# Layer 3 of a four-layer graph-attention kernel: V's parts side by side in the value matmuls, their sum on DVE, column vectors made in the node stages, and ACT making the kinks of three tiles of four

## The chip, the core and the metric

The program runs on one core of a Trainium2 chip. Its engines are PE (matrix products), DVE (vector), ACT (scalar functions), POOL (GpSimd) and SP, which here only issues DMAs. The metric is the time of one execution on the device, in microseconds; a kernel's time is the median of several executions.

## The reference

Eight graphs of 1024 nodes with 128 features pass through four attention layers under one adjacency matrix; after each layer `x = layernorm(x + layer(x))`. Layers 0 and 1 are dot-product attention with four heads, layers 2 and 3 additive attention. The change is about layer 3 (four heads of 32 features):

```python
Wh = jnp.einsum('bnf,hfd->bhnd', x, W)
ei = jnp.einsum('bhnd,hd->bhn', Wh, a1)
ej = jnp.einsum('bhnd,hd->bhn', Wh, a2)
e = ei[:, :, :, None] + ej[:, :, None, :]
e = jnp.where(e > 0, e, ALPHA * e)          # ALPHA = 0.2
e = jnp.where(adj[None, None] > 0, e, MASK_VAL)
att = jax.nn.softmax(e, axis=-1)
h = jnp.einsum('bhij,bhjd->bhid', att, Wh)
return jax.nn.elu(h)                         # after the heads are joined
```

Layer 2 is the same with one head of 128 features. The `where(e > 0, ...)` is what this text calls the kink.

## The kernel before

**Stages.** The program goes through five node stages (`node(0)` to `node(4)`) with the attention of a layer (`heads(0)` to `heads(3)`) between them. Each engine has its own program in one block, in the order of the stages; semaphores join them, and nothing reorders at run time. A node stage works graph by graph: it finishes the layer behind, and projects for the layer ahead. For layers 2 and 3 it writes to DRAM, per graph, V in three bf16 parts (`v_d`, each part 32 features and a one, 33 columns), rows of `ei` (`row_d`) and columns of `ei` and `ej` (`col_d`). In `project`, DVE copies the columns from PSUM bank 4 in one operation (line 1309), and the next graph's transposes on PE wait for that.

**Attention.** `heads(layer)` runs over 32 units (graph and head) in layer 3. The body holds four units, so eight passes are made; the first and the last stand outside the loop. A unit has 16 tiles of 128 keys x 512 queries: two halves of queries (c), eight key blocks (j) in each. Per tile s:

- PE, `scores(s)`: a mask matmul (lines 1063 or 1068) and the matmul with `sel` (line 1070) into PSUM bank s % 4. It adds the shift of each query, which lies as a row in `qs`.
- The kink. For tiles with s % 4 in `RELU_AT[3]`, now 1 and 3, ACT writes `relu(0.8 (ei + ej))` into the bank before PE adds to it (`relu`, line 849), right behind the exponential that has read this bank. For the others DVE makes it afterwards, in `settle(s)` (line 1402): bank to `arg` (named cv in rows).
- ACT, `exps(s)` (line 875): the exponential into `part`, from cv or from the bank (ps).
- POOL, `take_low(s)` (line 332): the low half of the probability as f16 (named xc), `part` read as bf16 being the high half.
- PE, `weigh(s - 6)`: for each of four query blocks, three matmuls of the high half and two of the low half with the parts of V, 33 columns each, added into one place of 33 columns (line 1111): 20 matmuls a tile. After the last tile of a half three more per block add V's sum for rows without neighbours (line 1118).

**Once per unit.** DVE takes eight row maxima of masked scores (`take_max`, line 1370) for the units ahead, spread over the tiles by `MAX_NEXT` and `MAX_AFTER`: at tiles 1, 2 and 7, 9, 11, 13, 14, 15. At tile 4, behind settle, `find_shift` makes the next unit's shift (lines 1346, 1347) and three scaled column vectors `colx` (1348 to 1350), which settle and ACT read as operands. At tiles 6 and 14 `half_done` (1451 to 1457) waits for `weigh` of tile 15 of the unit behind or tile 7, and normalizes half a unit. SP stores a unit's output after its second half_done (line 548), then copies the next shift into `qs` with eight DMAs (`place_shift`, line 533), then loads a unit ahead with nine DMAs (line 497).

Of the kernel before, what the change touches and what calls it, by code (L numbers as in the profile page):

```python
# [25 lines left out]
F32 = mybir.dt.float32  # L26
# [4 lines left out]
ALU = mybir.AluOpType  # L31
# [3 lines left out]
P = 128  # L35
# [35 lines left out]
RELU_AT = ((), (), (1, 3), (1, 3))  # L71
# [4 lines left out]
LOADS = (9, 7, 6, 9)  # L76
# [3 lines left out]
HCHAIN = (36, 32, 52, 28)  # L80
HLEFT = (7, 4, 6, 3)
# [6 lines left out]
def build(nc, t):  # L88
    with ExitStack() as ctx:
# [18 lines left out]
        col_d = nc.dram_tensor("col_d", (GRAPHS * 8, P, BLOCKS), F32, kind="Internal").ap()  # L108
# [46 lines left out]
        colp = sb("colp", [P, 8, BLOCKS])  # L155
# [17 lines left out]
        cols = sb("cols", [P, UNROLL, 2, BLOCKS])  # L173
        colx = sb("colx", [P, UNROLL, 3, BLOCKS])
# [49 lines left out]
        s_colx = sem("s_colx")  # L224
# [110 lines left out]
        def settled_before(layer, u, s):  # L335

            if layer == 0:
                return u * (TILES // 2 * UNROLL) + s // 2
            return TILES // 2 * UNITS[0] + TILES // 2 * (UNIT0[layer] - UNIT0[2]) + u * (TILES // 2 * UNROLL) + s // 2

        def arg_at(s):
            return s // 2 % RING
# [44 lines left out]
        def _(sp):  # L387
# [31 lines left out]
            def node(stage):  # L419
# [17 lines left out]
                def store_parts(b):  # L437
# [7 lines left out]
                    else:  # L445
                        n = 2 * HEADS[stage]
                        sp.wait_ge(s_ev["row2"], ev("row2", stage, b))
                        for kind in range(4):
# [3 lines left out]
                        sp.dma_start(col_d[bass.ds(b * 8, n)].rearrange("r p t -> p r t"), colp[:, 0:n, :]  # L452
                                     ).then_inc(s_pst[q], 16)
# [35 lines left out]
            def load_unit(layer, u, m):  # L489
# [16 lines left out]
                else:  # L506
# [10 lines left out]
                    for k in range(2):  # L517
                        go(cols[:, n, k, :], one(col_d, r + k * heads).rearrange("a p t -> (a p) t"))
# [210 lines left out]
        def _(act):  # L729
# [95 lines left out]
            def first_relu(layer):  # L825
                act.wait_ge(s_stk[0], stk_at(layer, 0, 0))
                act.wait_ge(s_colx, UNIT0[layer] - UNIT0[2] + 1)
                for s in RELU_AT[layer]:
                    act.activation(ps[:, s, :], si8[:, 0, 0:HALF], ACT.Relu, bias=colx[:, 0, 1, s:s + 1]
                                   ).then_inc(s_relu, 1)  # L830

            def heads(layer):
                def body(u, first, last):
# [6 lines left out]
                    def relu(s):  # L840
# [3 lines left out]
                        if s % TILES == RELU_AT[layer][0]:  # L844
                            act.wait_ge(s_stk[slot], stk_at(layer, slot, u + n // UNROLL))
                            act.wait_ge(s_colx, UNIT0[layer] - UNIT0[2] + u * UNROLL + n + 1)
# [3 lines left out]
                                       bias=colx[:, slot, 1, j:j + 1]).then_inc(s_relu, 1)  # L850
# [9 lines left out]
                    def exps(s):  # L860
# [4 lines left out]
                        elif s % RING in RELU_AT[layer]:  # L865
                            act.wait_ge(s_score, T - CREDIT + 1)
                            n, j = s // TILES, s % BLOCKS
                            src, more = ps[:, s % RING, :], dict(bias=colx[:, n, 2, j:j + 1])
                        else:
                            act.wait_ge(s_p, p_at(s))  # L870
                            n, j = s // TILES, s % BLOCKS
                            src, more = arg[:, arg_at(s), :], dict(bias=cols[:, n, 1, j:j + 1])
# [14 lines left out]
                if layer > 1:  # L887

                    act.wait_ge(s_open, 2 * layer - 2)
# [16 lines left out]
        def _(pe):  # L906
# [103 lines left out]
            def heads(layer):  # L1010
# [22 lines left out]
                def body(u, first, last):  # L1033
# [3 lines left out]
                    def scores(s):  # L1037
# [19 lines left out]
                        else:  # L1057

                            bank = ps[:, s % RING, :]
                            if s % RING in RELU_AT[layer]:  # L1060

                                pe.wait_ge(s_relu, settled_before(layer, u, s) - TILES // 2 * UNITS[0] + 1)
# [11 lines left out]
                    def weigh(s):  # L1074
# [14 lines left out]
                        for it in range(IB):  # L1089
                            if layer == 1:  # L1090
# [6 lines left out]
                                               skip_group_check=True)  # L1097
                                continue
# [6 lines left out]
                            else:  # L1105
                                acc = ps[:, 6 + c, it * width:(it + 1) * width]
                                opens = j == 0 and it == 0
# [77 lines left out]
        def _(dve):  # L1185
# [44 lines left out]
            def node(stage):  # L1230
# [52 lines left out]
                def project(b):  # L1283
# [16 lines left out]
                    else:  # L1300
# [8 lines left out]
                        dve.tensor_copy(colp[:, 0:n, :], ps[:, 4, 0:BLOCKS * n].rearrange("p (t r) -> p r t", r=n)  # L1309
                                        ).then_inc(s_ev["col"], 1)  # L1310
# [20 lines left out]
            def heads(layer):  # L1331
# [10 lines left out]
                def find_shift(n, U):  # L1342

                    m = nshift[:, n % 2, :]
                    z, col = shift[:, 0, :], cols[:, n, 1, :]
# [225 lines left out]
```

## Time and profile before

| | us |
|---|---|
| median of 3 runs | 2839.0 (2838.48 to 2839.67) |
| the profiled execution's own time | 2835.98 |
| its span, first to last instruction | 2834.1 |
| PE, DVE, ACT, POOL busy in the span | 2200.2, 2176.8, 1577.9, 1882.5 |
| attention of layer 3, 2105 to 2758 us of the span | 653 |
| in it PE, DVE, ACT, POOL busy | 566, 577, 497, 516 |
| node stage 3, 1950 to 2105 | 155 |

Busy time is the union of an engine's instructions; neighbouring instructions overlap, so an engine's pace is read from starts, not from durations. A unit's length is read as the distance of the same instruction in neighbouring units. In rows, `x8` is a count, a bracket at the end is idle time of the engine ahead of the row and what ended it, and "issue" is an end that no other engine explains.

### The profile page before, as it was taken

The numbers are of one execution on the slowest core, as the hardware profiler recorded it, in microseconds if no ns is written. First come the engines' busy times: TensorE is split into PE (matmuls) and PEld (weight loads), VectorE is DVE, ScalarE is ACT, GpSimd is POOL, SyncE is SP. The second block draws the span as 40 slices with busy tenths as digits, with TensorE's granted clock in tenths as the row PEclk, the third lists the DMA queues.
The fourth block names the chain that finished last, engine by engine and source line by source line (L and its number), as shares of the span: only waits on it lengthen the run. The fifth ranks groups of instructions, "written<-read, shape, count | busy, mean of one in ns | idle before, by whom it ended". The sixth has DMA issues, their size and how long they took to land.

```text
span 2834.1 us, 89438 instructions
## 1 busy us (share of the span) xinstructions
PE 2200.2 (78%) x32984; PEld 1571.2 (55%) x32984; DVE 2176.8 (77%) x4078; ACT 1577.9 (56%) x2273; POOL 1882.5 (66%) x1837
## 2 busy tenths in 40 slices
PE   4587888788566799999995775995649988888980
PEld 3366666666454355666663553884326666666660
DVE  4499999999666599999993336873759988888965
ACT  3354444445266255555553453664728777777776
POOL 2298888888644377887885344774218878778873
PEclk9788888888777799999997667997769999999995
DMA  6932233232266422222223643312631212111217
GB/s 240 325 91 75 68 81 80 64 79 63 52 194 208 118 65 65 65 64 64 64 65 81 170 136 117 103 51 97 153 99 42 53 43 53 47 49 44 54 36 163
DMA packets 337383, 267.68 MB, mean 94 GB/s; under 512 B 229840, under 2 KB 293584, under 8 KB 337056
## 3 DMA queue, kind: packets, MB, share of 16 engines
q1 hardware_dynamic: 332448, 246.12, 32.5%
q0 software_dynamic: 4608, 16.78, 1.6%
q8 instruction: 256, 4.19, 0.6%
q14 instruction: 71, 0.58, 0.1%
HBM read 167.13 MB, written 95.36 MB: 93 GB/s over the span
## 4 chain that ended last, share of the span: by engine, by line
PE 37%; issue 18%; DVE 18%; ACT 8%; SPq 7%; DMA 5%; POOL 2%; DVEq 1%; ACTq 0%; POOLq 0%
PE ps L1111 12%; SPq L533 5%; DVE xn L1428 4%; PE ps L1070 4%; DMA qs<-nshift 3%; PE ps L958 3%; ACT xn L738 3%; DVE full L1370 3%; DVE cv L1390 2%; PE ps L1051 2%; PE ps L1063 2%; PE ps L1068 2%; PE ps L1029 2%; PE ps L982 2%; PE ps L1054 2%
## 5 line engine op out<-in xcount | busy, mean ns | idle before, releaser
L332 POOL TENSOR_TENSOR xc<-part 128x512 f16<-128x512 f32 x1536 | 1633.0, 1094 | 473.6 <-ACT part L875 326.3
L1111 PE MATMUL ps<-vs,part 128*128 128x33 bf16 (+1 forms) x13824 | 823.5, 186 | 1.2 <-DVE work L1419 1.1
L1111 PEld LDWEIGHTS ps<-vs,part 128*128 128x128 bf16 x13824 | 658.5, 99 | 272.0 <-issue 202.7
L1111 PE MATMUL ps<-vs,xc 128*128 128x33 bf16 (+1 forms) x9216 | 762.1, 184 | 4.4 <-issue 4.4
L1370 DVE CUSTOM_DVE_ANT_0 full<-ps,mask_n 128x1024 bf16<-128x1024 f32 x512 | 618.4, 1218 | 88.5 <-DVE xn L1462 29.0
L1111 PEld LDWEIGHTS ps<-vs,xc 128*128 128x128 f16 x9216 | 583.2, 97 | 0.1
L857 ACT ACTIVATE part<-cv,lift 128x1024 f32<-128x1024 f32 x256 | 294.7, 1151 | 323.9 <-DVE cv L1390 297.0
L875 ACT ACTIVATE part<-ps 128x512 f32<-128x512 f32 x512 | 305.8, 598 | 281.9 <-PE ps L1055 281.9
L1051 PE MATMUL ps<-qs,ks 128*128 128x512 f32 x512 | 288.8, 567 | 122.8 <-DVE cv L1390 95.7
L1070 PE MATMUL ps<-qs,sel 128*128 128x512 f32 x640 | 380.1, 596 | 0.0
L1390 DVE SCALAR_TENSOR_TENSOR cv<-ps,mask_t 128x1024 f32<-128x1024 f32 x256 | 311.8, 1219 | 46.3 <-PE ps L1051 22.4
L875 ACT ACTIVATE part<-cv,cols 128x512 f32<-128x512 f32 x320 | 228.9, 715 | 200.5 <-DVE cv L1402 193.9
L1055 PE MATMUL ps<-qs,ks 97*128 97x512 f32 x512 | 301.7, 590 | 0.0
L1402 DVE SCALAR_TENSOR_TENSOR cv<-ks,colx,ps 128x512 f32<-128x512 f32 x320 | 238.2, 745 | 75.7 <-PE ps L1070 64.2
L1093 PEld LDWEIGHTS ps<-vs,part 128*128 128x128 bf16 x2048 | 161.0, 98 | 133.1 <-issue 96.3
L1093 PE MATMUL ps<-vs,part 128*128 128x99 bf16 x2048 | 229.6, 212 | 1.0 <-POOL xc L332 1.0
L849 ACT ACTIVATE ps<-ks,colx 128x512 f32<-128x512 f32 x316 | 218.7, 692 | 11.5
L875 ACT ACTIVATE part<-ps,colx 128x512 f32<-128x512 f32 x320 | 214.6, 671 | 3.4
L1095 PE MATMUL ps<-vs,xc 128*128 128x66 bf16 x2048 | 216.0, 194 | 0.0
L1054 PE MATMUL ps<-mask_t,ident_b 128*128 128x512 bf16 x512 | 198.2, 387 | 16.2 <-DMA qs<-nshift 10.4
L1029 PE MATMUL ps<-ks,qs 96*128 96x512 f32 x512 | 188.5, 451 | 21.7 <-DMA vs<-v_d 19.2
L1051 PEld LDWEIGHTS ps<-qs,ks 128*128 128x128 f32 x512 | 111.4, 218 | 132.0 <-DVE cv L1390 96.5
(147 smaller groups left out, 3413.8 us busy)
## 6 DMA issues: line engine op xcount, KB each, us to landing
qs<-q_d SPq DMA_DIRECT2D x224, 128.0 KB
ks<-k_d SPq DMA_DIRECT2D x224, 128.0 KB
ks<-row_d SPq DMA_DIRECT2D x40, 512.0 KB
vs<-v_d SPq DMA_DIRECT2D x96, 198.0 KB
q_d<-part SPq DMA_DIRECT2D x32, 512.0 KB
k_d<-part SPq DMA_DIRECT2D x32, 512.0 KB
ctx_d<-xn SPq DMA_DIRECT2D x96, 128.0 KB, 1.7
xc<-ctx_d SPq DMA_DIRECT2D x96, 128.0 KB, 4.4
```

The costliest lines, as they stand in the source:

```text
L332: eng.tensor_tensor(plo[:, r, :], prob[:, r, :], phi[:, r, :], ALU.subtract).then_inc(low_done(layer, u, s)[0], 1)
L857: act.activation(prob[:, r:r + 2, :], arg[:, a:a + 2, :], ACT.Exp, scale=2.0 * CLIP, bias=lift[:, 0:1]).then_inc(s_exp, 2)
L875: act.activation(prob[:, r, :], src, ACT.Exp, **more).then_inc(s_exp, 1)
L1029: mm = pe.matmul(ps[:, at + c, :], qs[0:96, n, k * P:(k + 1) * P], ks[0:96, n, c * HALF:(c + 1) * HALF], start=True, stop=True)
L1051: mm = pe.matmul(bank, ks[:, n, blk_j], qs[:, n, cut], start=True, stop=True)
L1054: pe.matmul(bank, ident_b[:, :], mask_t[:, j, cut], start=True, stop=False)
L1055: mm = pe.matmul(bank, ks[0:97, n, blk_j], qs[0:97, n, cut], start=False, stop=True)
L1070: mm = pe.matmul(bank, sel[:, 2, :], qs[:, n, cut], start=False, stop=True, skip_group_check=True)
L1093: pe.matmul(ps[:, 6 + c, at_a:at_a + V3], phi[:, r, it * P:(it + 1) * P], vs[:, n, at_v:at_v + V3], start=opens, stop=False, skip_group_ch ...
L1111: mm = pe.matmul(acc, half[:, r, it * P:(it + 1) * P], vs[:, n, at:at + width], start=opens and h == 0 and v == 0, stop=h == 1 and v == 1, ...
L1370: dve.tensor_tensor_reduce(junks[k % 2], src, mask_n[:, k, :], 1.0, least, ALU.add, ALU.max, accum_out=dst).then_inc(s_nmax, 1)
L1390: dve.scalar_tensor_tensor(arg[:, a:a + 2, :], ps[:, r:r + 2, :], -0.5, mask_t[:, j:j + 2, c * HALF:(c + 1) * HALF], ALU.max, ALU.min).the ...
```

## The change

In layer 3 alone, if not said otherwise:

1. `weigh` multiplies each half of a probability block with all parts of V side by side: one matmul of 99 columns and one of 66, into three places of 33 columns, as layer 1 does; eight matmuls a tile in place of 20, and one in place of three for the empty rows.
2. `half_done` multiplies all three places by the reciprocal and sums them (the branch of layer 1), two operations in place of one, four links in its chain in place of three (`HCHAIN`, `HLEFT`).
3. `RELU_AT[3]` is (1, 2, 3): ACT makes the kinks of three tiles of four, DVE settles only tiles with s % 4 = 0. The counts that PE, DVE and ACT wait for, and the place in `arg`, follow from that.
4. For layers 2 and 3 the scaled columns come from the node stage: DVE there writes five columns per head (two copies, three products) in place of one copy, `col_d` holds them side by side, one DMA per unit loads all five (`LOADS` one lower), and `find_shift` keeps only the shift. `colx` and its semaphore go.

```diff
-RELU_AT = ((), (), (1, 3), (1, 3))
+RELU_AT = ((), (), (1, 3), (1, 2, 3))
-LOADS = (9, 7, 6, 9)
+LOADS = (9, 7, 5, 8)
...
-                    for k in range(2):
-                        go(cols[:, n, k, :], one(col_d, r + k * heads).rearrange("a p t -> (a p) t"))
+                    go(cols[:, n, :, :], one(col_d, g).rearrange("a p k t -> (a p) k t"))
...
                         act.activation(ps[:, s % RING, :], si8[:, slot, c * HALF:(c + 1) * HALF], ACT.Relu,
-                                       bias=colx[:, slot, 1, j:j + 1]).then_inc(s_relu, 1)
+                                       bias=cols[:, slot, 3, j:j + 1]).then_inc(s_relu, 1)
...
                         for it in range(IB):
-                            if layer == 1:
+                            if layer in (1, 3):
...
                                 mm = pe.matmul(ps[:, 6 + c, at_a:at_a + 66], plo[:, r, it * P:(it + 1) * P],
                                                vs[:, n, at_v:at_v + 66], start=False, stop=True,
                                                skip_group_check=True)
+                                if layer == 3 and j == BLOCKS - 1:
+                                    at_i = c * HALF + it * P
+                                    mm = pe.matmul(ps[:, 6 + c, at_a:at_a + V3], empty[:, at_i:at_i + P], zs[:, n, :],
+                                                   start=False, stop=True, skip_group_check=True)
                                 continue
...
-                            if layer == 3 and j == BLOCKS - 1:
-
-                                at_i = c * HALF + it * P
-                                for v in range(3):
-                                    mm = pe.matmul(acc, empty[:, at_i:at_i + P], zs[:, n, v * 33:(v + 1) * 33],
-                                                   start=False, stop=v == 2, skip_group_check=True)
...
-                        dve.tensor_copy(colp[:, 0:n, :], ps[:, 4, 0:BLOCKS * n].rearrange("p (t r) -> p r t", r=n)
-                                        ).then_inc(s_ev["col"], 1)
+                        heads = HEADS[stage]
+                        got = ps[:, 4, 0:BLOCKS * n].rearrange("p (t k h) -> p h k t", k=2, h=heads)
+                        for k in range(2):
+                            dve.tensor_copy(colp[:, 0:heads, k, :], got[:, :, k, :])
+                        dve.tensor_scalar(colp[:, 0:heads, 2, :], got[:, :, 1, :], SLOPE - 1.0, None, ALU.mult)
+                        dve.tensor_scalar(colp[:, 0:heads, 3, :], got[:, :, 1, :], 1.0 - SLOPE, None, ALU.mult)
+                        dve.tensor_scalar(colp[:, 0:heads, 4, :], got[:, :, 1, :], SLOPE, None, ALU.mult
+                                          ).then_inc(s_ev["col"], 1)
...
-                    dve.scalar_tensor_tensor(colx[:, n, 0, :], col, SLOPE, col, ALU.mult, ALU.subtract)
-                    dve.scalar_tensor_tensor(colx[:, n, 1, :], col, -SLOPE, col, ALU.mult, ALU.add)
-                    dve.scalar_tensor_tensor(colx[:, n, 2, :], col, SLOPE - 1.0, col, ALU.mult, ALU.add
-                                             ).then_inc(s_colx, 1)
...
-                            parts = 3 if layer == 1 else 1
+                            parts = 1 if layer == 2 else 3
```

On ACT, at the start of layer 3's attention (cv: what DVE has settled; ps: a PSUM bank; ks: the row of `ei`). Before:

```order
L802 ACTIVATE vs<-cv 128x32x32
L829 ACTIVATE ps<-ks,colx 128x512 x2
L875 ACTIVATE part<-cv,cols 128x512
L875 ACTIVATE part<-ps,colx 128x512
L849 ACTIVATE ps<-ks,colx 128x512
```

Now:

```order
L814 ACTIVATE vs<-cv 128x32x32
L840 ACTIVATE ps<-ks,cols 128x512 x3
L885 ACTIVATE part<-cv,cols 128x512
L885 ACTIVATE part<-ps,cols 128x512
L859 ACTIVATE ps<-ks,cols 128x512
L885 ACTIVATE part<-ps,cols 128x512
L859 ACTIVATE ps<-ks,cols 128x512
L885 ACTIVATE part<-ps,cols 128x512
L859 ACTIVATE ps<-ks,cols 128x512
```

What came once in three rows, a kink, comes three times in seven, and two of the three stand ahead of an exponential from ps.

On DVE, in a unit of layer 3, from tile 4's settle (cv) to the maximum of tile 7. Before:

```order
L1402 SCALAR_TENSOR_TENSOR cv<-ks,colx,ps 128x512
L1346 SCALAR_TENSOR_TENSOR shift<-top,cols 128x8
L1347 SCALAR_TENSOR_TENSOR nshift<-shift 128x8
L1348 SCALAR_TENSOR_TENSOR colx<-cols 128x8
L1349 SCALAR_TENSOR_TENSOR colx<-cols 128x8
L1350 SCALAR_TENSOR_TENSOR colx<-cols 128x8
L1402 SCALAR_TENSOR_TENSOR cv<-ks,colx,ps 128x512
L1451 TENSOR_SCALAR rden<-ps 128x4
L1452 RECIPROCAL rden<-rden 128x4
L1457 TENSOR_TENSOR xn<-ps,rden 128x128
L1370 ISA full,top<-ps,mask_n 128x1024
```

Now:

```order
L1409 SCALAR_TENSOR_TENSOR cv<-ks,cols,ps 128x512
L1357 SCALAR_TENSOR_TENSOR shift<-top,cols 128x8
L1358 SCALAR_TENSOR_TENSOR nshift<-shift 128x8
L1458 TENSOR_SCALAR rden<-ps 128x4
L1459 RECIPROCAL rden<-rden 128x4
L1467 TENSOR_TENSOR work<-ps,rden 128x384
L1469 TENSOR_REDUCE xn<-work 128x128
L1377 ISA full,top<-ps,mask_n 128x1024
```

The settle of tile 6 and the three `colx` operations are gone from between the shift and half_done, and half_done's product is three times as wide with a sum behind it.

## Rows read from the trace of the kernel before

**Rows 1.** Busy us of each engine by stretch, then clock, DMA share, GB/s.

```profile
500.00:520.00 20.00, 15.66 (x322) 12.10 (x318) 16.09 (x24) 8.47 (x8) 15.87 (x16) 0.74 0.29 72
1735.00:1950.00 215.00, 210.12 (x2816) 175.93 (x2816) 158.56 (x299) 128.82 (x190) 163.20 (x143) 0.98 0.21 67
2500.00:2600.00 100.00, 86.61 (x1867) 62.22 (x1865) 90.87 (x174) 77.32 (x121) 80.27 (x80) 0.98 0.19 46
2441.00:2446.00 5.00, 5.00 (x68) 3.11 (x68) 2.83 (x5) 2.07 (x4) 2.04 (x2) 0.50 0.15 44
```

**Rows 2.** Order of time (start us, us, line, operation): DVE's shift ticks, layer 3.

```profile
2128.96 0.25 DVE L1346 SCALAR_TENSOR_TENSOR shift<-top,cols 128x8 f32<-128x8 f32 x1
...
2406.09 0.24 DVE L1346 SCALAR_TENSOR_TENSOR shift<-top,cols 128x8 f32<-128x8 f32 x1
...
2425.53 0.24 DVE L1346 SCALAR_TENSOR_TENSOR shift<-top,cols 128x8 f32<-128x8 f32 x1
...
2704.98 0.25 DVE L1346 SCALAR_TENSOR_TENSOR shift<-top,cols 128x8 f32<-128x8 f32 x1
```

**Rows 3.** Order of time, DVE, inside one unit of layer 3.

```profile
2406.37 0.96 DVE L1347 SCALAR_TENSOR_TENSOR nshift<-shift 128x8 f32<-128x8 f32 x1
...
2408.55 0.75 DVE L1402 SCALAR_TENSOR_TENSOR cv<-ks,colx,ps 128x512 f32<-128x512 f32 x1
...
2410.47 1.23 DVE L1370 CUSTOM_DVE_ANT_0 full<-ps,mask_n 128x1024 bf16<-128x1024 f32 x1 [0.56 <-DVE xn L1457]
...
2411.62 0.74 DVE L1402 SCALAR_TENSOR_TENSOR cv<-ks,colx,ps 128x512 f32<-128x512 f32 x1
2412.28 1.22 DVE L1370 CUSTOM_DVE_ANT_0 full<-ps,mask_n 128x1024 bf16<-128x1024 f32 x1
```

**Rows 4.** Order of time, ACT, layer 3; last, its waits, 2200 to 2700.

```profile
2404.43 0.71 ACT L875 ACTIVATE part<-cv,cols 128x512 f32<-128x512 f32 x1
2405.05 0.67 ACT L875 ACTIVATE part<-ps,colx 128x512 f32<-128x512 f32 x1
2405.74 0.69 ACT L849 ACTIVATE ps<-ks,colx 128x512 f32<-128x512 f32 x1
2406.37 0.71 ACT L875 ACTIVATE part<-cv,cols 128x512 f32<-128x512 f32 x1
...
2750.86 0.72 ACT L875 ACTIVATE part<-cv,cols 128x512 f32<-128x512 f32 x1 [0.93 <-DVE cv L1402]
...
ACT part L875 <- DVE cv L1402: 100.5, 80, 4.6
```

**Rows 5.** Order of time, POOL and PE, in the same unit.

```profile
2413.28 8.04 POOL L332 TENSOR_TENSOR xc<-part 128x512 f16<-128x512 f32 x8 [1.02 <-ACT part L875]
...
2418.25 0.39 PE L1068 MATMUL ps<-mask_t,ident_b 128*128 128x512 bf16 x1 [0.33 <-DMA qs<-nshift]
```

**Rows 6.** Order of time, PE: tiles of layers 1 and 3, a pass end.

```profile
1493.18 0.38 PE L1054 MATMUL ps<-mask_t,ident_b 128*128 128x512 bf16 x1
...
1493.95 0.38 PE L1054 MATMUL ps<-mask_t,ident_b 128*128 128x512 bf16 x1
...
2400.79 0.58 PE L1070 MATMUL ps<-qs,sel 128*128 128x512 f32 x1
...
2401.76 0.59 PE L1070 MATMUL ps<-qs,sel 128*128 128x512 f32 x1
...
2440.99 0.61 PE L1068 MATMUL ps<-mask_t,ident_b 128*128 128x512 bf16 x1 [3.61 <-issue]
...
2442.46 0.59 PE L1063 MATMUL ps<-mask_t,ident_b 128*128 128x512 bf16 x1
```

**Rows 7.** Order of time, DVE, layer 1: half_done's first operation, and what follows.

```profile
1305.44 0.15 DVE L1451 TENSOR_SCALAR rden<-ps 128x4 f32<-128x4 f32 x1
...
1307.58 1.23 DVE L1370 CUSTOM_DVE_ANT_0 full<-ps,mask_n 128x1024 bf16<-128x1024 f32 x1 [0.56 <-DVE xn L1462]
```

**Rows 8.** Order of time, DVE, node stage 3: one graph's column copy.

```profile
2076.99 0.20 DVE L1309 COPY colp<-ps 128x64 f32<-128x64 f32 x1
```

More of the change, by code:

```diff
@@ L154, in build @@
         vsumb = sb("vsumb", [P, 4, 3, 33], BF16)
[L155 removed]
+        colp = sb("colp", [P, 4, 5, BLOCKS])
         qs = sb("qs", [P, UNROLL, NODES], F32R)
@@ L172, in build @@
         zs = sb("zs", [P, UNROLL, V3], BF16)
-        cols = sb("cols", [P, UNROLL, 2, BLOCKS])
-        colx = sb("colx", [P, UNROLL, 3, BLOCKS])
+        cols = sb("cols", [P, UNROLL, 5, BLOCKS])
         flat = part[:, :, :, :, :].rearrange("p g a b n -> p (g a b n)").bitcast(F32)
@@ L338, in settled_before, with kinks_before, arg_at @@
                 return u * (TILES // 2 * UNROLL) + s // 2
-            return TILES // 2 * UNITS[0] + TILES // 2 * (UNIT0[layer] - UNIT0[2]) + u * (TILES // 2 * UNROLL) + s // 2
-        def arg_at(s):
-            return s // 2 % RING
+            own = [r for r in range(RING) if r not in RELU_AT[layer]]
+            before_layer = TILES // 2 * UNITS[0] + sum(
+                TILES // RING * (RING - len(RELU_AT[m])) * UNITS[m] for m in range(2, layer))
+            return before_layer + u * (TILES // RING * len(own) * UNROLL) + s // RING * len(own) + sum(
+                r < s % RING for r in own)
+        def kinks_before(layer, u, s):
+            own = RELU_AT[layer]
+            return sum(TILES // RING * len(RELU_AT[m]) * UNITS[m] for m in range(2, layer)) + (
+                u * (TILES // RING * len(own) * UNROLL) + s // RING * len(own) + sum(r < s % RING for r in own))
+        def arg_at(layer, s):
+            if layer == 0:
+                return s // 2 % RING
+            return (s // RING * (RING - len(RELU_AT[layer])) + sum(
+                r < s % RING for r in range(RING) if r not in RELU_AT[layer])) % RING
         def stored_before(layer, u, n):
@@ L826, in first_relu @@
                 act.wait_ge(s_stk[0], stk_at(layer, 0, 0))
-                act.wait_ge(s_colx, UNIT0[layer] - UNIT0[2] + 1)
                 for s in RELU_AT[layer]:
-                    act.activation(ps[:, s, :], si8[:, 0, 0:HALF], ACT.Relu, bias=colx[:, 0, 1, s:s + 1]
+                    act.activation(ps[:, s, :], si8[:, 0, 0:HALF], ACT.Relu, bias=cols[:, 0, 3, s:s + 1]
                                    ).then_inc(s_relu, 1)
@@ L867, in exps @@
                             n, j = s // TILES, s % BLOCKS
-                            src, more = ps[:, s % RING, :], dict(bias=colx[:, n, 2, j:j + 1])
+                            src, more = ps[:, s % RING, :], dict(bias=cols[:, n, 4, j:j + 1])
                         else:
@@ L871, in exps @@
                             n, j = s // TILES, s % BLOCKS
-                            src, more = arg[:, arg_at(s), :], dict(bias=cols[:, n, 1, j:j + 1])
+                            src, more = arg[:, arg_at(layer, s), :], dict(bias=cols[:, n, 1, j:j + 1])
                         act.wait_ge(s_av, T - DEEP + 1)
@@ L887, in heads @@
                 if layer > 1:
-                    act.wait_ge(s_open, 2 * layer - 2)
+                    act.wait_ge(s_open, sum(len(RELU_AT[m]) for m in range(layer + 1)))
                     first_relu(layer)
@@ L1401, in settle @@
                         dve.wait_ge(s_exp, T - 2 * RING + 1)
-                        dve.scalar_tensor_tensor(arg[:, arg_at(s), :], si8[:, n, c * HALF:(c + 1) * HALF],
-                                                 colx[:, n, 0, j:j + 1], ps[:, s % RING, :], ALU.max, ALU.add
+                        dve.scalar_tensor_tensor(arg[:, arg_at(layer, s), :], si8[:, n, c * HALF:(c + 1) * HALF],
+                                                 cols[:, n, 2, j:j + 1], ps[:, s % RING, :], ALU.max, ALU.add
                                                  ).then_inc(s_p, 1)
@@ L1455, in half_done @@
                             scale = rden[:, 0:blocks].unsqueeze(2)
-                            if layer > 1:
+                            if layer == 2:
                                 link(dve.tensor_tensor(o, acc[:, :, 0, 0:width],
```

22 lines of the change are left out of this document (9 added, 13 removed).

## The prediction

> **What bounds the kernel now.** I read the busy time by stretch first, then the order of time of each engine inside the attention of layer 3, the only loop whose order the change rewrites. There PE, DVE, ACT and POOL are all busy for 77 to 91 us of 100, DVE most [rows 1], so shares decide nothing and the loop has to be timed. It runs over 32 units of 16 tiles. Its clock tick is the pair of small shift operations that DVE makes once per unit: two of them in undisturbed units stand 19.44 us apart, and 29 units, from the second to the thirty-first tick, take 576.0 us [rows 2]. 29 x 19.44 is 563.8; the other 12 us come at the places where one pass of the loop of four units ends and the next begins: PE stands there for 3.61 us [rows 6] and then works for a while at a granted clock near 0.5 (1.2 GHz) [rows 1].
>
> Inside a unit DVE has no free time: a settle step is 0.66 us (start to start), a row-maximum step 1.15, the shift group 2.46, half_done 1.26 with its gap [rows 3], and they follow one another. ACT, in contrast, waits for DVE's settles again and again, 100.5 us in 500 [rows 4]. So DVE's 19.44 us is the unit. A second ring is almost as long: half_done at tile 6, store of the output, eight shift copies on SP's queue, landing, first scores of the next unit at 2418.25, which waited for them, 8.3 us after half_done's end (0.56 ahead of 2410.47, so 2409.91) [rows 3, 5].
>
> **DVE, part by part.** Four of eight settles per unit go: 4 x 0.66 = 2.64 us off. The three colx operations go: DVE's shift ends at 2407.33 (2406.37 + 0.96) and the next settle starts at 2408.55 [rows 3]; of these 1.22 us I keep 0.1 for the wait on its own shift, 1.1 off. half_done gets the threefold product and the sum. Layer 1 has just this form: 1305.44 to 1307.58, 2.14 us with the gap behind [rows 7], against 1.26 now: 0.88 more, twice a unit, 1.76 on. DVE's unit: 19.44 - 2.64 - 1.1 + 1.76 = 17.5 us. DVE gains 1.9 us and stops being the longest.
>
> **ACT.** Now four tiles cost four exponentials and two kinks; afterwards four and three. Steps, start to start: exponential from cv to the next 0.62, exponential from ps to a kink 0.69 (the kink writes the bank that the exponential has just read, so it waits for its end), kink to exponential from cv 0.63 [rows 4]. No row shows a kink followed by an exponential from ps, which will happen twice in four tiles. The nearest row is the 0.63 behind a kink; the other end is no overlap at all, 0.70 from the kink's own 0.69 [rows 4]. I take 0.63: four tiles cost 0.62 + 3 x 0.69 + 3 x 0.63 = 4.58 us, a unit 18.3; with 0.70 it is 4.72 and 18.9. Now it is 4 x 3.88 = 15.5. So ACT becomes the longest engine, 1.1 us below today's unit.
>
> The Trainium skill, "ScalarE: Activation LUTs", section "What ACT_TABLE_LOAD costs", says that back-to-back activations overlap by about 93 ns; by that figure the unseen step would be an estimated 0.60 us, the unit 18.1 and the total some 7 us lower than mine.
>
> **The others.** POOL makes eight low parts in 8.04 us [rows 5], 16.1 a unit, unchanged. PE's tile shrinks: now the second wide matmul of one tile and of the next stand 0.97 us apart; in layer 1, whose tile has two wide matmuls of the same size and the eight value matmuls of 99 and 66 columns, tiles start 0.77 apart [rows 6]. That is 12.3 us a unit, some 13.3 with the spread and empty-row matmuls: PE's gain is hidden behind ACT. The ring over SP: from the first scores of a unit to DVE's first settle 0.65 (an estimate: its second wide matmul alone takes 0.58 [rows 6]), then settle, two maxima, settle, shift group without colx and half_done without its gap, 0.66 + 2.5 + 0.66 + 1.36 + 1.58 = 6.8, then 8.3: 15.7 us. It was tied with DVE; it falls below ACT. One column load of two leaves SP's queue per unit; SP is not late except through that ring, so it counts nothing.
>
> **Can DVE keep ACT fed?** Its work is in lumps. A settle can start some 1.45 us after the kink before it (0.45 scores, 0.32 values, 0.65 until the scores are there, by the 0.77 us tile [rows 6]) and must be done, 0.75 later, when ACT needs it 4.58 us after that kink: DVE may run ahead by about 2.4 us. Its longest stretch between two settles is tiles 12 to 16: settle, two maxima, half_done, a maximum, 0.66 + 2.3 + 2.14 + 1.15 = 6.25, 1.67 over ACT's 4.58. Tiles 4 to 8 take 5.3, 0.7 over. The two stretches between them take about 3.0 each and give it back. So it fits, with 0.7 us to spare.
>
> **Sum.** 29 units at 18.32 are 531.3 us. For the pass ends I keep 15 us, near today's 12 (ends: nothing, and seven times 3.61 = 25): 546.3 against 576.0, 29.7 saved. The last 42 tiles, most of them without maxima on DVE, now take 45.9 us (2704.98 to 2750.86 [rows 2, 4]); at ACT's 1.145 they take 48.1: 2.2 lost. The last half_done loses 0.9. The start of the layer loses a load and three colx operations: 0.6 saved. In the node stages DVE makes five small column operations in place of one copy of 0.20 us [rows 8]; each has half its elements or fewer, so five of them lie between five times 0.1 and five times 0.2 (estimates from that row), less the 0.2: 0.3 to 0.8 more a graph, I take 0.45. Where ACT and PE set the pace it costs nothing, where the next transposes wait for the columns it counts; between none and all eight graphs of stage 3 (0 to 6.4 us) I take half of eight, 1.8. Layer 2, which keeps two kinks of four, gets only shorter shift groups on DVE, beside a PE that is busy 210 of its 215 us [rows 1]: nothing, and at most 8 x 1.1 = 9 us saved if DVE mattered.
>
> Net: -29.7 + 2.2 + 0.9 - 0.6 + 1.8 = -25.4 us. The profiled execution took 2836.0 us (span 2834.1), 3.0 below the median; 2810.6 for it, 2814 as a median.
>
> **Rivals.** *The lumps stop ACT (slower).* If DVE cannot run ahead, say because a half_done waits for values that PE has not yet made, each stretch costs the longer of ACT's and DVE's: 4.58 + 5.3 + 4.58 + 6.25 = 20.7 us, 2.4 over my unit: 29 x 2.4 = 69 us, 2883. It decides against the change from a unit of about 19.4 us on, when half of the run-ahead is lost. For it: ACT's 100.5 us of waits for settles [rows 4]. Against: these are the slack of an engine with 15.5 us of work in 19.44. I give it 6 in 100, and 11 to a loss of a third to a half of the run-ahead: a unit of 19.0 to 19.4, 2834 to 2845, no change.
>
> *ACT's new pairs do not overlap.* 18.9 a unit, 29 x 0.56 = 16 us, 2830; still faster. 15 in 100.
>
> *PE's clock falls (slower).* PE is left with short waits in each tile. Layer 3 now has the clock at 0.98 with PE busy 87 us of 100, layer 0 at 0.74 in 20 us with PE busy 15.7 [rows 1]. At the lower level (1.2 GHz) today's tile is 1.47 us against 0.97 [rows 6]; the new one would lie between 0.77 x 1.47 / 0.97 = 1.17 and twice 0.77, say 1.45. ACT needs 1.145 a tile, so PE sets the unit only when the clock is low for more than about half the time. At three quarters it is 16 x 1.28 + 1 = 21.5 us, 29 x 3.2 = 93 us, 2907. Layer 3 as it is keeps 0.98 in 100 us [rows 1] although PE waits for kinks in it too, and a PE that sets the pace is busy without a break, as it was behind the pass end, from where the clock did come back: 3 in 100. The Trainium skill, "TensorE: Matmul & The Clock Gate", section "A second HAM failure mode: psum-queue depth-cycling", speaks for this rival: frequent small idle times between groups of matmuls make the clock swing between its levels. The trace so far bears it out in layer 0 alone.
>
> **How the numbers follow.** The forecast, ACT's 18.3 us and 2814, has 65 in 100. With the pairs that don't overlap, 80 in 100 lie below 2833, faster by more than 0.2% (5.7 us, about what a measurement of this kernel can tell from no change); 11 within; 9 slower. The range: downwards a shorter unseen step (7 us) and cheaper pass ends (7 us), 2800; upwards through the pairs and most of the lost run-ahead, 2842.
>
> **What would show it.** Right: the shift ticks 18.3 us apart; ACT's idle before exponentials from cv almost gone, ACT busy over 90 of 100 us; DVE busy below its 91 and waiting for scores; PE waiting for kinks in three tiles of four at a clock near 1. Wrong: kinks and exponentials 0.70 apart; ACT still waiting for settles over 1 us at tiles 0 and 8; PE clock well under 0.9 in the layer; a pass end that costs much over 2 us; node stage 3 longer by over 4 us.

## The result, and the profile after

The changed kernel takes 2799.9 us (median of 4 runs, 2796.0 to 2802.4) against 2839.3 for the kernel before beside it: ratio 0.9858, 95% interval 0.9841 to 0.9875, so 1.4% faster. I had forecast 2814 with a range from 2800 to 2842: right in direction and in what becomes the longest engine, some 14 us too high, and the median lies just below the range. The profiled executions, which the rest compares, took 2799.0 and 2836.0 us (spans 2797.3 and 2834.1), 37 apart.

The first view is the busy time by stretch, two of the stretches of [rows 1]: busy us of PE, PEld, DVE, ACT and POOL with their counts, then the granted clock.

```profile
2500.00:2600.00 100.00, 82.82 (x916) 50.42 (x932) 89.00 (x161) 97.85 (x153) 88.86 (x88) 1.00 0.19 48
2441.00:2446.00 5.00, 4.33 (x45) 2.59 (x47) 4.12 (x8) 4.90 (x9) 4.47 (x5) 1.00 0.05 16
```

ACT is busy 97.85 us of 100 where it was 77.32 [rows 1]. The clock is 1.00, though PE now waits in most tiles. ACT in order of time, four tiles from one exponential from cv to the next, answers to [rows 4]:

```profile
2402.20 0.71 ACT L885 ACTIVATE part<-cv,cols 128x512 f32<-128x512 f32 x1
2402.82 0.67 ACT L885 ACTIVATE part<-ps,cols 128x512 f32<-128x512 f32 x1
2403.51 0.69 ACT L859 ACTIVATE ps<-ks,cols 128x512 f32<-128x512 f32 x1
2404.14 0.67 ACT L885 ACTIVATE part<-ps,cols 128x512 f32<-128x512 f32 x1
2404.84 0.69 ACT L859 ACTIVATE ps<-ks,cols 128x512 f32<-128x512 f32 x1
2405.47 0.67 ACT L885 ACTIVATE part<-ps,cols 128x512 f32<-128x512 f32 x1
2406.17 0.69 ACT L859 ACTIVATE ps<-ks,cols 128x512 f32<-128x512 f32 x1
2406.80 0.71 ACT L885 ACTIVATE part<-cv,cols 128x512 f32<-128x512 f32 x1
```

No row has a bracket, so ACT does not wait in these four tiles. The steps are 0.62, then 0.69 or 0.70 and 0.63 in turn: the step that no row of before had shown, a kink to an exponential from ps, is 0.63 (2403.51 to 2404.14). Four tiles take 4.60 us, a unit 18.4. In the list of waits from 2200 to 2650 ACT has no entry any more (it waited 100.5 us for settles [rows 4]); it is now the others that wait for ACT (engine and line, what it waited for: us, times, longest):

```profile
PEld ps L1073 <- ACT ps L859: 111.9, 268, 0.5
PE ps L1073 <- ACT ps L859: 59.7, 194, 0.4
...
POOL xc L331 <- ACT part L885: 51.5, 196, 0.4
...
DVE cv L1409 <- PE ps L1080: 11.9, 25, 0.5
```

DVE's shift ticks, as in [rows 2]: the second, two on either side of a pass end, and the thirty-first.

```profile
2128.89 0.87 DVE L1357 SCALAR_TENSOR_TENSOR shift<-top,cols 128x8 f32<-128x8 f32 x1
...
2404.58 0.46 DVE L1357 SCALAR_TENSOR_TENSOR shift<-top,cols 128x8 f32<-128x8 f32 x1
...
2423.04 0.49 DVE L1357 SCALAR_TENSOR_TENSOR shift<-top,cols 128x8 f32<-128x8 f32 x1
...
2662.14 0.58 DVE L1357 SCALAR_TENSOR_TENSOR shift<-top,cols 128x8 f32<-128x8 f32 x1
```

The 29 units take 533.25 us against 576.0, and that is 29 x 18.39. All distances but the first (17.8) lie between 18.3 and 18.5, the one over the pass end (2404.58 to 2423.04, 18.46) too. Before, the distance at the same place was 22.7 us. So the pass ends, for which I had kept 15 us, cost nothing. On PE, the first tile of that pass (the mask matmul of line 1078) now begins like this; in [rows 6] its mask matmul stood behind 3.61 us of stop:

```profile
2416.16 0.58 PE L1080 MATMUL ps<-qs,sel 128*128 128x512 f32 x1
...
2416.95 0.39 PE L1078 MATMUL ps<-mask_t,ident_b 128*128 128x512 bf16 x1
2416.98 0.58 PE L1080 MATMUL ps<-qs,sel 128*128 128x512 f32 x1
```

Looking at all pass ends of before again, there are five stops, not seven: they end at 2279.49, 2360.71, 2440.99, 2521.43 and 2602.37, after 4.98, 3.33, 3.61, 3.49 and 3.39 us. The loop makes six of the eight passes, so it jumps back five times; where it is entered and left, code runs straight on and nothing stops.

The view of DMA queues has a line for the queue that loads instructions: packets, MB, share. In the whole attention of layer 3, before and then after:

```profile
q8 instruction: 106, 1.74, 1.1%
```

```profile
q8 instruction: 17, 0.28, 0.2%
```

A packet is 16.4 KB (1.74 MB / 106). Before, 106 packets are 13 for each of eight passes, and the single pass from 2280 to 2361 shows 13; one of them starts within the stop that ends at 2440.99. After, 17 are 5.7 for each of the three places where a pass stands in the program: 11 come before 2268, in the first pass and the first one of the loop, 6 after 2640, in the last pass, and from 2268 to 2640, with all five jumps back, there is none.

### The profile page after: what moved, and what is told of

Same layout as the page of the kernel before. It is cut to its first block, busy times and chain, and to the rows that moved or that the text cites. A ratio compares the mean times of both kernels' runs of the same rounds, so it can differ in the third digit from the quotient of the medians.

```text
span 2797.3 us, 75685 instructions
## 1 busy us (share of the span) xinstructions
PE 2126.2 (76%) x26087; PEld 1462.0 (52%) x26329; DVE 2127.4 (76%) x3958; ACT 1658.2 (59%) x2401; POOL 1879.6 (67%) x1837
## 4 chain that ended last, share of the span: by engine, by line
PE 27%; issue 24%; DVE 16%; ACT 14%; SPq 5%; POOL 4%; DMA 4%; DVEq 1%; ACTq 1%; POOLq 0%
ACT part L885 9%; PE ps L1122 7%; DVE xn L1435 4%; SPq L545 4%; POOL xc L331 3%; PE ps L1061 3%; PE ps L968 2%; DVE cv L1397 2%; ACT xn L750 2%; PE ps L1039 2%; PE ps L1065 2%; DVE full L1377 2%; DMA qs<-nshift 2%; PE ps L1080 2%; PE ps L992 2%
## 5 line engine op out<-in xcount | busy, mean ns | idle before, releaser
L1122 PE MATMUL ps<-vs,part 128*128 128x33 bf16 (+1 forms) x7680 | 489.5, 191 | 2.2 <-DVE work L1426 2.0
L1103 PE MATMUL ps<-vs,part 128*128 128x99 bf16 x4096 | 466.8, 211 | 2.8 <-POOL xc L331 2.7
L1103 PEld LDWEIGHTS ps<-vs,part 128*128 128x128 bf16 x4096 | 325.3, 98 | 268.4 <-issue 168.0
L1122 PEld LDWEIGHTS ps<-vs,part 128*128 128x128 bf16 x7680 | 386.2, 101 | 136.1 <-issue 76.4
L1122 PE MATMUL ps<-vs,xc 128*128 128x33 bf16 (+1 forms) x5120 | 449.3, 189 | 3.6 <-issue 3.6
L1105 PE MATMUL ps<-vs,xc 128*128 128x66 bf16 x4096 | 441.0, 194 | 0.0
L1105 PEld LDWEIGHTS ps<-vs,xc 128*128 128x128 f16 x4096 | 340.5, 99 | 0.0
L1122 PEld LDWEIGHTS ps<-vs,xc 128*128 128x128 f16 x5120 | 334.9, 98 | 0.0
L859 ACT ACTIVATE ps<-ks,cols 128x512 f32<-128x512 f32 x443 | 306.5, 692 | 15.3
L885 ACT ACTIVATE part<-ps,cols 128x512 f32<-128x512 f32 x448 | 299.9, 670 | 3.8
L1409 DVE SCALAR_TENSOR_TENSOR cv<-ks,cols,ps 128x512 f32<-128x512 f32 x192 | 143.2, 746 | 83.0 <-PE ps L1080 74.9
L1039 PE MATMUL ps<-ks,qs 96*128 96x512 f32 x512 | 188.2, 451 | 21.2 <-DMA vs<-v_d 18.7
L885 ACT ACTIVATE part<-cv,cols 128x512 f32<-128x512 f32 x192 | 136.7, 712 | 90.6 <-DVE cv L1409 90.5
```

The costliest lines, as they stand in the source:

```text
L859: act.activation(ps[:, s % RING, :], si8[:, slot, c * HALF:(c + 1) * HALF], ACT.Relu, bias=cols[:, slot, 3, j:j + 1]).then_inc(s_relu, 1)
L885: act.activation(prob[:, r, :], src, ACT.Exp, **more).then_inc(s_exp, 1)
L1103: pe.matmul(ps[:, 6 + c, at_a:at_a + V3], phi[:, r, it * P:(it + 1) * P], vs[:, n, at_v:at_v + V3], start=opens, stop=False, skip_group_ch ...
L1105: mm = pe.matmul(ps[:, 6 + c, at_a:at_a + 66], plo[:, r, it * P:(it + 1) * P], vs[:, n, at_v:at_v + 66], start=False, stop=True, skip_grou ...
L1122: mm = pe.matmul(acc, half[:, r, it * P:(it + 1) * P], vs[:, n, at:at + width], start=opens and h == 0 and v == 0, stop=h == 1 and v == 1, ...
```

## The experiments

**The theories.** A: the stop at the jump comes from the length of PE's loop body. Code that is too long to stay loaded is fetched anew in every pass, and at the jump back PE has to wait for it; eight value matmuls a tile in place of 20 make the body short enough. B: the stop is gone because PE, which works less than ACT now, comes to the jump early. Under B any change that leaves PE slack would do.

**The changed kernel with a long body.** Layer 3's value matmuls are cut into pieces that write the same three places (the edit in short; the matmuls for the empty rows are cut in the same way).

```diff
-  pe.matmul(acc[99 columns], high, v[99 columns]); pe.matmul(acc[66 columns], low, v[66 columns])
+  for v in range(3): pe.matmul(acc[33 columns of place v], high, v[33 columns of part v])
+  for v in range(2): pe.matmul(acc[33 columns of place v], low, v[33 columns of part v])
```

> The changed kernel with one thing different: in layer 3 each value matmul of 99 or 66 columns is cut into matmuls of 33 columns that write the same three places (20 a tile in place of 8, 12 in place of 4 for the empty rows), so PE's loop body has as many matmuls as before the change, while DVE, ACT and the data are those of the changed kernel. Theory A (length of PE's body: code that is fetched anew in every pass): the instruction queue moves about 106 packets in layer 3's attention as before the change, not 17 as after it; PE stops 3.3 to 3.6 us at the five jumps back; the five distances of the shift ticks that hold a jump grow by 2 to 5 us over 18.4, and the time is 2810 to 2825. Rival B (lead: PE works less than ACT and so comes to the jump early, whatever its code): ticks stay 18.3 to 18.5 apart everywhere, 2797 to 2804.

It took 2824.5 us; ratio to the kernel before 0.9938 (0.9921 to 0.9955). The instruction queue, PE at a jump, ACT behind it, and PE's clock in the 5 us after:

```profile
q8 instruction: 106, 1.74, 1.1%
```

```profile
2439.83 0.61 PE L1078 MATMUL ps<-mask_t,ident_b 128*128 128x512 bf16 x1 [4.22 <-issue]
2439.87 0.99 PE L1080 MATMUL ps<-qs,sel 128*128 128x512 f32 x1
```

```profile
2438.32 0.69 ACT L859 ACTIVATE ps<-ks,cols 128x512 f32<-128x512 f32 x1
2441.86 0.72 ACT L885 ACTIVATE part<-cv,cols 128x512 f32<-128x512 f32 x1 [2.84 <-DVE cv L1415]
```

```profile
2439.80:2444.80 5.00, 4.97 (x68) 3.12 (x68) 3.03 (x5) 2.87 (x5) 2.06 (x3) 0.50 0.02 3
```

All five stops are back, 3.7 to 4.3 us, although PE (busy 515.1 us of the 554.5 of the 29 units) works less than ACT (524.1). That goes against B, though PE's lead is small here; a run with a larger one follows below (two places). After the stop the clock is at its lower level (0.50, 1.2 GHz). The ticks over a jump are 22.5 to 23.8 us apart, all others 18.0 to 18.6; the 29 units take 554.5 us, 21.3 more than in the changed kernel, 4.3 a jump. That is the larger part of the difference in time (24.6 us between the medians, 22.7 by the two ratios).

**The three parts, each alone in the kernel before.** The diff of the change is applied in part.

```diff
 kinks alone:    -RELU_AT = ((), (), (1, 3), (1, 3))
                 +RELU_AT = ((), (), (1, 3), (1, 2, 3))
 columns alone:  five columns from the node stages, colx gone, LOADS (9, 7, 5, 8)
 V side alone:   -if layer == 1:
                 +if layer in (1, 3):      and parts = 3 in half_done
```

> The kernel before with ACT making three kinks of four in layer 3, and nothing else of the change: V's parts one after another, colx as before. DVE's unit would be 19.44 - 2.64 = 16.8, ACT's 18.4 as after the change, PE's some 16.5. Theory A: ticks 18.4 apart inside a pass, five stops of PE of 3.3 to 3.6 us that cost 2 to 5 us each: the attention loop saves 43 less 10 to 25, time 2808 to 2823. Rival B: no excess at the jumps, 2797 to 2802.

> The kernel before with the five columns from the node stages and nothing else of the change. DVE's unit loses the 1.1 us of the colx operations: 18.3, ACT 15.5, PE 16.5. If the 1.1 us is right and theory A holds (body as long as before, ends cost the same 12 us): 29 x 1.1 = 32 saved, node stage 3 up to 6 us longer, 2805 to 2813. Rival B (PE now has 1.9 us of lead a unit, ends vanish): 2794 to 2800. If the small operations lay beside a wait that DVE has anyway: 2830 to 2842.

> The kernel before with V's parts side by side and DVE's sum, and nothing else of the change. DVE gets 2 x 0.88 us a unit more: 21.2; PE's tile falls to about 0.77. Both theories: no stops of PE at the jumps (A: the body is short, 17 packets on the instruction queue; B: PE has a lead of 7 us a unit). 29 x 21.2 = 615 against 576, last half_done 0.9: 2875 to 2882. If half_done's sum costs less than 0.88 in layer 3, below that.

| | time, us | ratio to before | 29 units, us | instruction packets | stops over 1.2 us without a releaser |
|---|---|---|---|---|---|
| before | 2841.3 | | 576.0 | 106 | 5 |
| kinks alone | 2821.5 | 0.9936 (0.9919 to 0.9952) | 552.4 | 106 | 5 |
| columns alone | 2811.8 | 0.9908 (0.9887 to 0.9929) | 548.7 | 106 | 5 |
| V side alone | 2881.5 | 1.0144 (1.0123 to 1.0165) | 617.9 | 17 | 0 |
| all three | 2799.9 | 0.9858 (0.9841 to 0.9875) | 533.3 | 17 | 0 |

The last row is the result's, against its own kernel before (2839.3). The five stops go with the body's length in every row. The kinks alone take the unit to ACT's 18.4 and the columns alone take it to 18.35, as expected from 19.44 less 1.1. In both the jumps cost more than the 12.3 us of before: 552.4 less 29 x 18.4 is 18.8, and 548.7 less 29 x 18.35 is 16.6. That these two parts together can't do much better than each alone, since ACT is then at its 18.4, is argued; the two weren't run together without the third. V side by side alone is 1.4% slower: the ticks stand mostly 21.2 to 21.9 apart, which is 19.44 and DVE's 1.76, and PE's short tile doesn't count. Its worth inside the change is the five stops: what costs 42 us alone removes, beside the other two, stops that cost 21 in the run with the long body.

The run with V's side alone also shows PE's clock falling in this layer without a jump: PE waits there for DVE and ACT, up to 1.7 us at a time. The 29 units, two such waits, and a stretch that begins within the second:

```profile
2128.93:2746.86 617.93, 472.02 (x4925) 294.07 (x4926) 572.72 (x1070) 450.62 (x697) 467.55 (x465) 0.90 0.17 43
```

```profile
2400.95 0.39 PE L1068 MATMUL ps<-mask_t,ident_b 128*128 128x512 bf16 x1 [1.30 <-DVE cv L1397]
...
2403.08 0.61 PE L1063 MATMUL ps<-mask_t,ident_b 128*128 128x512 bf16 x1 [1.19 <-ACT ps L849]
```

```profile
2402.70:2406.10 3.40, 3.02 (x22) 1.99 (x23) 3.15 (x7) 3.37 (x6) 3.40 (x5) 0.50 0.00 0
```

The clock is 0.90 on average and at its lower level in stretches like this one. As PE has slack there, this costs at most the 3 us by which the 29 units exceed 29 x 21.2 = 615.

**Where the limit lies.** 16 value matmuls a tile: the high part in three pieces, the low part in one.

> The changed kernel with layer 3's high part in three matmuls of 33 columns and the low part in one of 66: 16 value matmuls a tile, between the 8 of the changed kernel and the 20 of the kernel before, everything else as in the changed kernel. It brackets the length of PE's body from which on its code is fetched in every pass. If 16 is short enough: 17 packets or fewer on the instruction queue in layer 3's attention, no stops at the jumps, 2797 to 2804. If too long: some 80 packets, five stops of about 4 us, ticks over a jump of 22 to 24 us, 2815 to 2830. A partial answer (some packets in each pass, shorter stops) would mean that only what does not fit is fetched.

2821.5 us (one run), 92 packets, five stops of 3.8 to 6.2 us, 29 units in 555.0. That is the full cost again, and 92 is 11.5 for each of eight passes: a body that is somewhat too long is fetched in every pass, not only the part that doesn't fit; the expectation had some 80 packets.

**A kink less on ACT.** Tile 10 of each unit goes back to DVE; the counts follow (the edit in words).

```diff
-  ACT makes the kinks of tiles s % 4 in (1, 2, 3)
+  ACT makes the kinks of tiles s % 16 in (1, 2, 3, 5, 6, 7, 9, 11, 13, 14, 15)
```

> The changed kernel with ACT making 11 kinks of 16 in layer 3 in place of 12: tile 10 goes back to DVE's settle. By the steps of ACT in the changed kernel a kink costs 0.70 us: ACT 17.7 a unit. DVE by the prediction's sum 17.5 + 0.66 = 18.16. If that sum is right the unit is 18.2, 29 x 0.2 = 6 us off the changed kernel, 2791 to 2796. If DVE's real unit is longer than the sum (its lumps, waits for its own results), the unit stays at 18.4 or grows, 2799 to 2815.

2787.7 us, ratio to before 0.9810 (0.9791 to 0.9829), below the expected 2791 to 2796. The ticks are 17.9 to 18.2 apart, 18.06 on average inside a pass, where I had 18.16 for DVE and 17.7 for ACT. ACT waits again a little for settles, so the two engines are nearly level here.

**Ten kinks, V's parts one after another.**

> V's parts one after another as before the change (20 matmuls a tile, one place, no sum on DVE), the columns from the node stages, and ACT making 10 kinks of 16 (DVE settles tiles 0, 4, 6, 8, 12, 14). DVE: 17.5 - 1.76 + 2 x 0.66 = 17.1 a unit, ACT 16.3 to 17.0, PE 16.5. Theory A: five stops as in the run with the long body, 4.3 us each, so 29 x 17.1 + 21 = 517 us for the 29 units against 533 in the changed kernel: 2780 to 2790. If PE's 16.5 with the clock after each stop sets the pace: 17.6 or more, 2797 and over.

2801.0 us, ratio 0.9865 (0.9846 to 0.9884): no better than the changed kernel. The stops are there (3.2 to 3.7 us, 106 packets). But the units between them are 17.9 to 18.3 long, not 17.1. From 2287 to 2323, between two jumps, PE is busy 33.75 us of 36, ACT 33.71 and DVE 32.66, at a clock of 1.00. DVE's shift pair, in the run with 10 kinks and then in the one with 11:

```profile
2308.43 0.90 DVE L1364 SCALAR_TENSOR_TENSOR shift<-top,cols 128x8 f32<-128x8 f32 x1
2309.36 0.96 DVE L1365 SCALAR_TENSOR_TENSOR nshift<-shift 128x8 f32<-128x8 f32 x1
```

```profile
2308.89 0.90 DVE L1359 SCALAR_TENSOR_TENSOR shift<-top,cols 128x8 f32<-128x8 f32 x1
2309.82 0.17 DVE L1360 SCALAR_TENSOR_TENSOR nshift<-shift 128x8 f32<-128x8 f32 x1
```

1.86 against 1.07 us for the same two operations of eight elements a row. My sum had them at what they take in the kernel before, 1.21 us as a rule, so they account for some 0.65 of the 0.8 to 1.2 us that it missed. PE also waits in this run for the shift copies of the ring over SP, 13.7 us in 440, so what sets its unit stays open.

**Two places, 12 matmuls a tile.** The high part's third piece goes into the second place, so that DVE's product and sum shrink by a third; 11 kinks on ACT.

> The changed kernel with two places per query block in place of three (high part 66 columns, then its third part 33 columns into the second place, low part 66 columns: 12 value matmuls a tile) and 11 kinks of 16 on ACT. DVE's product and sum in half_done have two thirds of their elements: some 0.44 of the 0.88 us goes, twice a unit, DVE 18.16 - 0.88 = 17.3; ACT 17.7. If a body of 12 matmuls a tile is short enough to stay loaded: unit 17.7, 29 x 0.7 = 20 us off the changed kernel, 2776 to 2784. If it is too long, five stops of some 4 us give it back: 2796 to 2804.

2801.1 us, ratio 0.9860 (0.9841 to 0.9880). The second of the two cases: 73 packets (9.1 a pass), five stops of 4.3 to 5.1 us. Between them the unit is 17.3 to 17.7, expected was 17.7, and the five ticks of 22.3 to 23.1 give it all back: 536.2 us. The queue, a jump, and the 29 units:

```profile
q8 instruction: 73, 1.20, 0.8%
```

```profile
2421.86 0.60 PE L1081 MATMUL ps<-mask_t,ident_b 128*128 128x512 bf16 x1 [4.88 <-issue]
```

```profile
2130.62:2666.80 536.18, 462.70 (x7001) 300.33 (x7002) 462.48 (x896) 504.17 (x783) 470.26 (x464) 0.97 0.20 52
```

PE is busy 463 us of 536 and ACT 504: PE has a clear lead, and every stop is there, so B is refuted. A body of 5.7 packets (93 KB) stays loaded, and one that fetches 9.1 a pass (149 KB) doesn't.

The Trainium skill, "Runtime: NRT & Kernel Launch", section "Instruction fetch mechanics", gives PE's instruction memory as 128 KiB, refilled in blocks of 16 KiB, and says that a taken branch whose target lies outside the current window of two pages has to wait for a fetch. The runs agree with the first two: 16.4 KB a packet, a limit between 93 and 149 KB. With the third they agree only where the body doesn't fit: the jump back over 93 KB, more than five such pages, waits for nothing. The section also says that code is only streamed in sequence and that nothing is gained by locality; there too the runs say otherwise, for a body of 93 KB loops with no packet at all.

**Three kernels side by side, and DVE's sum first.** The changed kernel, the one with 11 kinks, and a version of the latter in which half_done sums out of PSUM before it multiplies (the edit in short):

```diff
-  work[128x384] = acc[128x384] * rden;  out = sum over places (work)
+  work[128x128] = sum over places (acc);  out = work * rden
```

> The changed kernel itself, as the standard for the two runs beside it on the same chip: 2796 to 2803, ticks 18.4 apart and none longer at the jumps.

> The run with 11 kinks of 16 on ACT again, beside the changed kernel: 9 to 13 us below it (its 29 units took 522.4 us against 533.3 in the first run). If the first result was the scatter of the stages ahead, less than 6.

> The run with 11 kinks on ACT, and in layer 3's half_done DVE sums the three places straight out of PSUM and multiplies the 128-wide sum by the reciprocal, in place of a 384-wide product (0.56 us) followed by the sum (0.59): the product falls to some 0.29, the width of the one in the kernel before. If DVE's work is the limit there (a unit of 18.0 where ACT's steps add up to 17.6 to 17.7), the unit falls to 17.6 to 17.7: 29 x 0.35 = 10 us below the run beside it, some 2778. If the wait for the sum, or ACT, already sets the unit, no change.

Medians of 2800.3, 2785.6 and 2793.3 us; ratios to before 0.9867 (0.9847 to 0.9886), 0.9828 (0.9804 to 0.9851) and 0.9838 (0.9819 to 0.9858). The first two repeat themselves: 11 kinks beat the changed kernel by some 12 to 15 us between medians, where 9 to 13 were expected. Two of the five runs of the second kernel lie at 2795.5, so the 10.8 us of the loop are the firmer figure: the 29 units take 522.4 against 533.3 in both pairs of profiles. That is the fastest version here.

The sum first was expected to gain 10 us; its 29 units take 528.7, 6.3 longer than without it. (Its median is 7.7 above that of the run beside it, but single runs of the two overlap.) Its two operations, at two places in one unit, and their durations (ns least/median/most):

```profile
2304.65 0.56 DVE L1471 TENSOR_REDUCE work<-ps 128x128 f32<-128x384 f32 x1
2305.24 1.17 DVE L1473 TENSOR_TENSOR xn<-work,rden 128x128 f32<-128x128 f32 x1
...
2313.39 0.56 DVE L1471 TENSOR_REDUCE work<-ps 128x128 f32<-128x384 f32 x1
2313.98 0.29 DVE L1473 TENSOR_TENSOR xn<-work,rden 128x128 f32<-128x128 f32 x1
```

```profile
L1473 DVE TENSOR_TENSOR xn<-work,rden x56: 291/292/1186, 2142.7 to 2643.2; 128x128 f32<-128x128 f32 x56
```

The sum from PSUM takes 0.56 as hoped, but the product, whose two inputs both lie in SBUF now, takes 0.29 or up to 1.19, on average 0.59, the price of the sum it replaces. POOL in the same stretches:

```profile
2304.22 4.28 POOL L331 TENSOR_TENSOR xc<-part 128x512 f16<-128x512 f32 x4 [0.33 <-ACT part L884]
...
2312.83 1.04 POOL L331 TENSOR_TENSOR xc<-part 128x512 f16<-128x512 f32 x1 [0.20 <-ACT part L884]
2314.20 2.04 POOL L331 TENSOR_TENSOR xc<-part 128x512 f16<-128x512 f32 x2 [0.33 <-ACT part L884]
```

The long product runs beside four low parts of POOL in a row, the short one starts in a gap between two (2313.87 to 2314.20). The shift pair of the same unit shows more closely what happens:

```profile
2309.60 3.04 POOL L331 TENSOR_TENSOR xc<-part 128x512 f16<-128x512 f32 x3 [1.10 <-ACT part L884]
```

```profile
2311.76 0.90 DVE L1359 SCALAR_TENSOR_TENSOR shift<-top,cols 128x8 f32<-128x8 f32 x1
2312.69 0.17 DVE L1360 SCALAR_TENSOR_TENSOR nshift<-shift 128x8 f32<-128x8 f32 x1
```

The first operation starts while POOL works and ends at 2312.66, 0.02 us after POOL's last low part (2312.64); the second starts in POOL's gap and takes 0.17. It is so in all 28 pairs of this run between 2140 and 2650: whatever starts beside a low part ends 0.02 us after it, whatever starts in a gap takes 0.17. The Trainium skill, "GPSIMD Engine Reference", section "8. Key points", says that GpSimd shares its SBUF interfaces with VectorE and is in conflict with DVE instructions with two SBUF inputs. The runs agree: the wider product out of PSUM that this one replaces took 0.556 to 0.559 us in all 57 cases. That the unit even grew by 0.2 us fits ACT's waits for settles, which rise from 7.1 to 12.4 us in 440; it wasn't tried apart.

## Why the prediction was wrong, and what of it held

Between the profiled executions, in us, minus is saved:

| term | forecast | measured |
|---|---|---|
| 29 units, without pass ends | 531.3 | 533.3 |
| pass ends | 15 | 0 |
| the same 29 units in all, against 576.0 | -29.7 | -42.8 |
| last units and last half_done | +3.1 | +5.2 |
| start of the layer | -0.6 | -2.3 |
| node stage 3 | +1.8 | +3.3 |
| all else | 0 | -0.4 |
| all | -25.4 | -37.0 |

**What held.** ACT becomes the longest engine, at 18.4 us a unit for a forecast of 18.3; the unseen step is 0.63 as taken, and the other end, 0.70, is refuted. The Trainium skill's 93 ns of overlap ("ScalarE: Activation LUTs", section "What ACT_TABLE_LOAD costs") would have made this step an estimated 0.60; the trace disagrees: the step is 0.63. DVE's terms held, each in a run of its own: the colx operations 1.1 (unit 18.35 with the columns alone), half_done 1.76 (21.2 with V alone), and one more settle makes the unit 18.06 against a sum of 18.16 (its shift pair takes 1.07 us there and not the 1.21 of the rows the sum is from, so that agreement is in part luck). PE's gain stays behind ACT. Layer 2 gains nothing: 234.8 and 235.8 us from its first scores to the first transposes behind it.

**The step that failed** is the term for the pass ends: 15 us kept, near the 12 of before, between the ends "nothing, and seven times 3.61" (the loop jumps back five times). They cost nothing. The range let them fall by only 7 us, which is why the time lies outside it. I treated the stop as a property of the loop, when it was one of the code in it, and the change shortens just that code: 13 packets a pass to 5.7. The run with the long body shows it from the other side: with all else of the change in place the stops are back and cost 21 us. The trace of before held the answer. Layer 1 runs the same loop with eight value matmuls a tile, and in its whole attention, 950 to 1525 us, the instruction queue has this line:

```profile
q8 instruction: 18, 0.29, 0.2%
```

PE has one stop over 1.2 us there for which the profile shows no releaser (3.33 us, in its last units, which no jump leads to), against five in layer 3. I read layer 1 for the length of a tile and not for its pass ends. Of the 11.6 us between the two sums the ends make 15; the unit and the tail, each 2 us longer than forecast, go the other way, so part of the error was hidden by luck.

**The smaller terms.** The tail is two longer than forecast. The last exponential from cv is tile 12's now, no longer tile 14's, so three tiles stand behind it where there was one. The two more, 0.57 us each, are some 1.1 of these 2 us:

```profile
2710.58 0.71 ACT L885 ACTIVATE part<-cv,cols 128x512 f32<-128x512 f32 x1
2711.19 1.82 ACT L885 ACTIVATE part<-ps,cols 128x512 f32<-128x512 f32 x3
```

In node stage 3 the five column operations start 0.1 us apart, the lower of the two estimates; the stage is 3.3 us longer (1970.96 to 2091.78, now 1969.93 to 2094.05), within the 0 to 6.4 that I had put. The other runs show that it is the columns: measured in the same way the stage takes 120.6 to 120.9 us in the three runs without them (before, kinks alone, V side alone) and 122.5 to 124.1 in the ten with them, so they cost 1.6 to 3.5 us.

**The rivals.** The lumps don't stop ACT: its waits for settles are gone. The pairs overlap. PE's clock doesn't fall in the changed kernel: it is 1.00 with PE busy 82.82 us of 100, and no wait of PE in the list above is longer than 0.5 us. The Trainium skill's rule on small idle times ("TensorE: Matmul & The Clock Gate", section "A second HAM failure mode: psum-queue depth-cycling") isn't borne out there. The rival isn't empty for this layer, though: with V's side alone the clock does swing between its levels, around waits of 1.0 to 1.7 us for other engines, and is 0.90 on average.

## What to carry to other kernels

A stop at the end of a loop's pass is a price of the code in the loop: look at the packets of the instruction queue per pass and compare a loop with fewer instructions, before such a stop is kept in a sum. Where one change moves several limits, its parts don't add up: each of the two that lowered the unit was worth 24 to 27 us of the attention alone, the third was a loss alone, and together they gave 43. When one engine has just become the longest, try handing a little back to the one relieved: one kink of twelve returned to DVE was worth some 11 us more.

## What the runs showed of the hardware

PE's loop of 93 KB of instructions (5.7 packets) runs without a fetch. Bodies that fetch 149 KB a pass or more do so in every pass, and PE stands 3.2 to 6.2 us at each jump back, then works at the lower clock level (0.50 in the 5 us looked at). With V's side alone the clock also goes to 0.50 around waits of PE of 1.0 to 1.7 us for other engines. DVE operations with both inputs in SBUF that start while POOL works take up to 0.9 us more: the product 0.29 to 1.19 us, the shift operations of eight elements 0.17 to 0.97, these ending 0.02 us after POOL's instruction. The wider product with an input from PSUM takes 0.556 to 0.559 us at all times.
